# Second layer of a four-layer kernel: probability transposes one projection later, a round's maxima in one run

## The reference

```python
q = hidden_state @ Wq + bq
k = encoder_hidden_state @ Wk + bk
v = encoder_hidden_state @ Wv + bv
...
scores = jnp.einsum('bkgld,bksd->bkgls', q, k) * scale
scores = scores + encoder_attention_mask[:, :, None, :, :]
attn = jax.nn.softmax(scores, axis=-1)
out = jnp.einsum('bkgls,bksd->bkgld', attn, v)
out = out.transpose(0, 3, 1, 2, 4).reshape(b, l, H)
out = out @ Wo + bo
x = out + hidden_state
mu = jnp.mean(x, axis=-1, keepdims=True)
var = jnp.var(x, axis=-1, keepdims=True)
return (x - mu) * jax.lax.rsqrt(var + EPS) * gamma + beta
```

## Time and profile before

| | us |
|---|---|
| median of 3 runs (2545.39 to 2549.48) | 2548.41 |
| the profiled execution | 2544.39 |
| its span, first to last instruction | 2542.4 |
| PE busy, share of the span | 2443.8 (96%) |
| POOL busy | 1125.3 (44%) |
| DVE busy | 1239.3 (49%) |
| ACT busy | 1088.3 (43%) |
| layer 1, from S1 of the first pass to S1 of the last | 331.28 |

### The profile page before, as it was taken

How to read it: one execution, slowest core, us unless ns; L and a number is a source line. 1 busy time by engine, 2 the same in 40 slices (tenths; PEclk the granted TensorE clock), 3 DMA queues, 4 the chain that set the end, 5 groups by cost and what they waited for, 6 DMA issues and landing times.

```text
span 2542.4 us, 48703 instructions
## 1 busy us (share of the span) xinstructions
PE 2443.8 (96%) x18464; PEld 2046.0 (80%) x18464; DVE 1239.3 (49%) x3296; ACT 1088.3 (43%) x3712; POOL 1125.3 (44%) x1972
## 2 busy tenths in 40 slices
PE   7999999999999999998888999999999999999999
PEld 6888887888888878886777788888888888788887
DVE  5565656323224667666666332233555555432332
ACT  5555554111114877877767111112555555211111
POOL 3444435600053787778877630033345433740000
PEclk9999999999999999998999999999999999999999
DMA  4121212311033223323443320122122111330100
GB/s 158 65 67 60 93 42 84 96 50 50 8 104 126 99 82 126 111 82 124 156 155 121 116 91 7 44 92 71 35 71 72 51 51 51 104 100 1 50 34 17
DMA packets 106774, 198.07 MB, mean 78 GB/s; under 512 B 8304, under 2 KB 35632, under 8 KB 103600
## 3 DMA queue, kind: packets, MB, share of 16 engines
q1 hardware_dynamic: 106544, 194.97, 22.8%
HBM read 136.22 MB, written 58.72 MB: 77 GB/s over the span
## 4 chain that ended last, share of the span: by engine, by line
PE 76%; ACT 11%; DVE 6%; POOL 4%; DMA 2%; issue 1%; SPq 0%; DVEq 0%; POOLq 0%
PE banks L327 68%; ACT plain_high L743 5%; PE banks L468 5%; PE banks L498 3%; ACT plain_low L743 2%; POOL plain_high L1372 2%; ACT plain_work L808 1%; DVE stats L1152 1%; DVE neg_max L1026 1%; PE banks L522 1%; ACT plain_work L727 1%; DMA plain_work<-mlp_w 1%; POOL plain_low L1372 0%; POOL rounded_high L318 0%; DMA plain_high<-attention_w 0%
## 5 line engine op out<-in xcount | busy, mean ns | idle before, releaser
L327 PE MATMUL banks<-rounded_work,rounded_low 128*128 128x512 f32 (+1 forms) x2688 | 531.9, 354 | 10.4 <-DVE rounded_low L1184 8.8
L327 PEld LDWEIGHTS banks<-rounded_work,rounded_low 128*128 128x128 f32 x2688 | 444.1, 198 | 74.8 <-issue 13.8
L836 ACT ACTIVATE plain_work<-banks,columns 128x512 f32<-128x512 f32 x192 | 132.4, 690 | 862.8 <-PE banks L327 856.5
L327 PE MATMUL banks<-rounded_work,rounded_high 128*128 128x512 f32 (+1 forms) x2400 | 479.4, 353 | 1.4 <-DMA rounded_work<-ctx_split 1.1
L327 PEld LDWEIGHTS banks<-rounded_work,rounded_high 128*128 128x128 f32 x2400 | 393.7, 189 | 66.1 <-issue 4.9
L1341 DVE CAST rounded_work<-plain_work 128x512 fp32r<-128x512 f32 x192 | 104.5, 544 | 683.9 <-ACT plain_work L836 669.4
L1372 POOL TENSOR_SCALAR plain_high<-plain_high,inv_sum 128x128 f32<-128x128 f32 (+1 forms) x768 | 297.9, 413 | 303.8 <-DVE inv_sum L1044 303.4
L327 PE MATMUL banks<-rounded_low,rounded_work 128*128 128x512 f32 x1728 | 416.1, 392 | 0.0
L327 PE MATMUL banks<-rounded_high,rounded_work 128*128 128x512 f32 (+1 forms) x1728 | 391.5, 378 | 1.7 <-DVE rounded_work L1343 1.7
L327 PEld LDWEIGHTS banks<-rounded_low,rounded_work 128*128 128x128 f32 x1728 | 321.5, 188 | 70.5 <-issue 4.4
L327 PEld LDWEIGHTS banks<-rounded_high,rounded_work 128*128 128x128 f32 x1728 | 308.9, 188 | 64.5 <-issue 5.0
(11 more groups left out here) (106 smaller groups left out, 3120.2 us busy)
## 6 DMA issues: line engine op xcount, KB each, us to landing
plain_work<-x SPq DMA_DIRECT2D x96, 256.0 KB, 3.0
plain_work<-mlp_w SPq DMA_DIRECT2D x96, 256.0 KB, 2.7
rounded_work<-ctx_split SPq DMA_DIRECT2D x16, 1024.0 KB, 5.7
u<-plain_work SPq DMA_DIRECT2D x48, 256.0 KB, 2.1
plain_work<-u SPq DMA_DIRECT2D x12, 1024.0 KB, 7.0
x<-plain_work SPq DMA_DIRECT2D x48, 256.0 KB, 2.2
plain_work<-attention_w SPq DMA_DIRECT2D x44, 256.0 KB, 2.7
ctx_split<-rounded_work SPq DMA_DIRECT2D x8, 1024.0 KB, 5.6
```

What stands on the lines that cost most here:

```text
L327: mm = pe.matmul(dst, lhs(i), rhs(j), start=first and n == 0, stop=last and n == 2, skip_group_check=True)
L836: act.activation(gelu[:, j % 2, :], bank(key), ACT.Gelu_apprx_tanh, bias=col(m.y, 28 + j)).then_inc(evac_of(key), 1)
```

## The change

It rewrites the order within a pass of layer 1 on PE, ACT, DVE and SP; no instruction is added or removed, apart from where waits stand.

On PE each T stands one projection further behind the scores: between the scores that precede it and T there is now an output projection or a projection to layer 2's values, and behind T, before its A, stand the keys or queries. The wait for the next pair's rows moves from the keys to the queries, which read them. On DVE the four maxima of a round run together, the copies of the older round's banks 1 and 3 come behind the inversion of the first two sums, and the inversion of the last two comes last. On ACT the copies of banks 0 and 2 move behind the exponentials of r = 1 and r = 2. The evacuation of X, keys and queries moves with PE's order. On SP the next context is loaded at the end of a pass, behind VG, instead of at the start of the next behind VC1.

```diff
+        def pe_rows(pe, y, p):
+            for i in range(2):
+                wait_evac(pe, ("X", y.n, p, i))
...
             for p in range(PAIRS):
                 more = p + 1 < PAIRS
                 pe_scores(pe, y, p, 1)
+                if p:
+                    pe_out(pe, y, 2 * p - 1)
                 pe_turn_probs(pe, y, p, 0)
                 pe_turn_x(pe, *((y, p + 1) if more else (L[2], 0)))
-                if p:
-                    pe_out(pe, y, 2 * p - 1)
+                if more:
+                    pe_keys(pe, y, p + 1, 0)
                 pe_attend(pe, y, p, 0)
                 if more:
-                    pe_keys(pe, y, p + 1, 0)
                     pe_keys(pe, L[2], p + 1, 0)
                 pe_scores(pe, y, p, 2)
+                if more:
+                    pe_values(pe, L[2], p + 1, 0)
                 pe_turn_probs(pe, y, p, 1)
                 pe_queries(pe, *((y, p + 1) if more else (L[2], 0)), 0)
-                if more:
-                    pe_keys(pe, L[2], p + 1, 1)
                 pe_attend(pe, y, p, 1)
                 pe_scores(pe, y, p, 3)
+                if more:
+                    pe_values(pe, L[2], p + 1, 1)
                 pe_turn_probs(pe, y, p, 2)
                 if more:
-                    pe_values(pe, y, p + 1, 0)
-                    pe_values(pe, L[2], p + 1, 0)
+                    pe_keys(pe, L[2], p + 1, 1)
...
                 pe_attend(pe, y, p, 2)
                 if more:
-                    pe_scores(pe, y, p + 1, 0)
-                else:
-                    pe_scores(pe, L[2], 0, 0)
+                    pe_values(pe, y, p + 1, 0)
+                pe_scores(pe, *((y, p + 1) if more else (L[2], 0)), 0)
+                pe_out(pe, y, 2 * p)
                 pe_turn_probs(pe, y, p, 3)
...
+        def act_late_round(act, y, p, k, turned, beside, of):
+
+            act_exp(act, y, p, k, 0)
+            beside()
+            act_exp(act, y, p, k, 1)
+            act_probs(act, of, *turned, 0)
+            act_exp(act, y, p, k, 2)
+            act_probs(act, of, *turned, 2)
+            act_exp(act, y, p, k, 3)
...
+        def dve_late_round(dve, y, p, k, turned, beside, behind, of):
+            for r in range(4):
+                dve_max(dve, y, p, k, r)
+            beside()
+            dve_invert(dve, y, p, k, (0,))
+            dve_probs(dve, of, *turned, 1)
+            dve_probs(dve, of, *turned, 3)
+            behind()
+            dve_invert(dve, y, p, k, (1,))
...
+                dve_late_round(dve, y, p, 1, (p, 0), odd_out, odd_moments, y)
+                for i in range(2):
+                    dve_x(dve, *((y, p + 1) if more else (L[2], 0)), i)
...
+                dve_late_round(dve, y, p, 3, (p, 2), second_values, nothing, y)
...
                 if more:
-                    sp_keys_ahead(sp, p + 1)
+                    sp_ahead(sp, p + 1)
+                if far:
+                    wait_filled(sp, ("V", 1, p + 1, 0))
+                    sp_c(sp, y, p + 2)
```

More of the change, by code:

```diff
@@ L350, in pe_inputs @@
                 pe.wait_ge(c_loaded, 16 * (c_index(y, p) + 1))
-                wait_evac(pe, ("X", y.n, p, 0))
-                wait_evac(pe, ("X", y.n, p, 1))
+                if y.kind == LATENT:
+                    pe_rows(pe, y, p)
+        def pe_rows(pe, y, p):
+            for i in range(2):
+                wait_evac(pe, ("X", y.n, p, i))
         def pe_turn_x(pe, y, p):
@@ L391, in pe_queries @@
                 pe_inputs(pe, y, p)
+            if y.kind == GQA and i == 0:
+                pe_rows(pe, y, p)
             x_t = XT_C if y.kind == CROSS else XC[:, :, :, 2 * P:4 * P]
@@ L1034, in dve_probs, with dve_invert @@
             dve_copy(dve, ("T", y.round(p, k), r), prob_t(y)[:, r, :])
-        def dve_invert(dve, y, p, k):
+        def dve_invert(dve, y, p, k, halves=(0, 1)):
             R, u = y.round(p, k), y.use(p, k)
-            for half in range(2):
+            for half in halves:
                 for r in (2 * half, 2 * half + 1):
@@ L1167, in dve_out, with dve_added @@
             dve.tensor_tensor(hidden[:, b % 2, :], bank(key), hidden[:, b % 2, :], ALU.add).then_inc(evac_of(key), 1)
-            wait_evac(dve, key)
+        def dve_added(dve, y, b):
+            wait_evac(dve, ("out", y.n, b))
             dve_moments(dve, y, b)
+        def dve_out(dve, y, b):
+            dve_add(dve, y, b)
+            dve_added(dve, y, b)
         def dve_again(dve, y, b):
@@ L1254, in dve_gqa, with odd_out, odd_moments, again @@
             dve.wait_ge(m_stored, 64 * GROUPS)
+            dve_values(dve, L[2], 0, 1)
             for p in range(PAIRS):
                 more = p + 1 < PAIRS
-                def inputs():
-                    for i in range(2):
-                        dve_x(dve, *((y, p + 1) if more else (L[2], 0)), i)
-                def next_inputs():
-                    if not more:
-                        for i in range(2):
-                            dve_x(dve, L[2], 1, i)
-                dve_values(dve, L[2], p, 1)
-                dve_round(dve, y, p, 1, (p, 0), inputs)
-                if p:
-                    dve_again(dve, y, 2 * p - 2)
-                    dve_out(dve, y, 2 * p - 1)
+                def odd_out():
+                    if p:
+                        dve_add(dve, y, 2 * p - 1)
+                def odd_moments():
+                    if p:
+                        dve_again(dve, y, 2 * p - 2)
+                        dve_added(dve, y, 2 * p - 1)
+                def again():
+                    if p:
+                        dve_again(dve, y, 2 * p - 1)
+                def second_values():
+                    if more:
+                        dve_values(dve, L[2], p + 1, 1)
+                dve_late_round(dve, y, p, 1, (p, 0), odd_out, odd_moments, y)
+                for i in range(2):
+                    dve_x(dve, *((y, p + 1) if more else (L[2], 0)), i)
+                if more:
+                    dve_keys(dve, y, p + 1, 0)
                 dve_heads(dve, y, p, 0)
                 if more:
-                    dve_keys(dve, y, p + 1, 0)
                     dve_keys(dve, L[2], p + 1, 0)
-                dve_round(dve, y, p, 2, (p, 1), nothing)
-                if p:
-                    dve_again(dve, y, 2 * p - 1)
+                dve_late_round(dve, y, p, 2, (p, 1), nothing, again, y)
                 dve_queries(dve, *((y, p + 1) if more else (L[2], 0)), 0)
+                dve_heads(dve, y, p, 1)
+                dve_late_round(dve, y, p, 3, (p, 2), second_values, nothing, y)
                 if more:
                     dve_keys(dve, L[2], p + 1, 1)
-                dve_heads(dve, y, p, 1)
-                dve_round(dve, y, p, 3, (p, 2), nothing)
-                if not more:
+                else:
                     dve_mask(dve, L[2], 0)
@@ L1287, in dve_gqa @@
                 dve_heads(dve, y, p, 2)
-                dve_round(dve, *((y, p + 1) if more else (L[2], 0)), 0, (p, 3), nothing, y)
-                next_inputs()
-                dve_out(dve, y, 2 * p)
+                dve_late_round(dve, *((y, p + 1) if more else (L[2], 0)), 0, (p, 3), lambda: dve_add(dve, y, 2 * p),
+                               lambda: dve_added(dve, y, 2 * p), y)
                 if more:
                     dve_queries(dve, y, p + 1, 1)
+                else:
+                    for i in range(2):
+                        dve_x(dve, L[2], 1, i)
                 dve_heads(dve, y, p, 3)
@@ L1675, in sp_gqa @@
             sp_ahead(sp, 0)
+            wait_filled(sp, ("V", 2, 0, 1))
+            sp_c(sp, y, 1)
             for p in range(PAIRS):
@@ L1686, in sp_gqa @@
                 if not more:
-                    wait_filled(sp, ("V", 2, p, 1))
+                    wait_filled(sp, ("Q", 1, p, 1))
                     sp_cross_keys(sp, 0)
```

54 lines of the change are left out of this document (23 added, 31 removed).

## The result

The changed kernel takes 2553.24 us (2549.87 to 2555.11) against 2546.27 (2541.89 to 2549.48) of the kernel before, timed with it: a ratio of 1.0030, 95% interval 1.0021 to 1.0039, some 7 us slower. The forecast was +3.6, the range held the time, and of the three chances the one that came true is "slower by over 0.2%", to which I had given 0.33.

The account below looks back on a forecast made before the run. PE was taken as the bound, with gaps from waits for POOL, DVE and ACT. Six passes +0.9, first pass +2.7 and last pass 0 gave +3.6 us: 2548.0, or 2552.0 on the runs' scale (+0.14%), range 2541 to 2560.

Parts of the forecast that it names:

- The links: Prices of steps between engines in a pass, each from one row, such as 0.72 us from ACT's copy to PE's matmul.
- the ledger: One full pass timed from S0 along PE, ACT and DVE: waits sum to 3.6 us, the pass to 47.65.
- A full pass: Layer 1's six full passes: waits exchanged for waits, 47.65 against 47.53 us, +0.1 each, +0.9 in six.
- The sum of 44.1: PE's work without waits in a full pass, 44.1 us, leaving at most 3.4 to gain from 47.53.
- half the bank waits vanish: Full passes: DVE or ACT catch up sooner than the priced steps say; 10.8 us off, 2541; chance 0.14.
- ACT, which copies T late, takes its place: Full passes: the softmax chain is hidden and ACT's late copies hold PE instead; +0.1 us a pass.
- First pass: Layer 1's first pass: X waits 3.05 us, A0 falls behind KG, the clock falls once; +2.7 us.
- The loss of clock: First pass: one fall of the granted clock behind the wait ahead of X, 1.1 to 1.9 us, taken as 1.5.
- The turn to layer 2: Last pass: Q0's lateness set against T3's lost POOL wait and earlier evacuations; 0, bounds -3.0 and +4.4 us.
- the step on SP: Context load behind VG, 18 us ahead of the next KG for a transfer of 5.7; no price.
- The rival in which it falls in every pass: Granted clock falls at KG or Q0's wait in each pass; +7 to +11 us, 2559 to 2563; chance 0.13.
- That transposes don't count as busy in the same way: Skill's rule, by which every pass would start KG at the low clock; given a small chance, since a row disagreed.

Follow-up runs that it names:

- Experiment 1: The changed kernel with ACT copying T0's bank 2 and T1's bank 0 one row of exponentials earlier; ratio 1.0016 to the kernel before.
- experiment 4: The changed kernel with the last pass in its old order on PE, ACT and DVE; ratio 1.0020 to the kernel before.
- experiment 2: The changed kernel with round 1 of the first pass in its old order, A0 ahead of KG; ratio 1.0015 to the kernel before.
- experiment 6: The changed kernel with DVE's copy of T's bank 1 again between the second and third maximum; ratio 1.0293 to the kernel before.
- experiments 1 to 4: Four variants of the changed kernel: early ACT copies 1.0016, old first-pass order 1.0015, layer 2's values loaded ahead of second keys 1.0013, old last-pass order 1.0020.
- experiment 5: The changed kernel with early ACT copies, X evacuated earlier, maxima ahead of evacuations in rounds 2 and 3, VC1 copied earlier; 2532.55 us, 0.9954 to the kernel before.

## Why the prediction came out as it did

**The links were right.** With S0 at 0, the ledger put KG at 18.15, Q0 at 30.7, T2's r = 3 at 40.3 and KC1 at 40.95; they stand at 18.07, 30.82, 40.42 and 40.99 (from S0 at 896.49). T no longer waits for POOL, and PE waits for ACT's copies in front of Q0 (1.33, forecast 1.4), KG (0.98, forecast 0.65) and for heads in front of O (0.69, forecast 0.75; the view calls it issue). Q1's wait of 0.1 and KC1's of 0.2 don't show.

**A full pass, +0.1 forecast, +0.34 measured.** The term that was mis-sized is the work between the waits, 44.59 where I had 44.1, more than the waits, which sum to 3.28, forecast 3.6. I took 2.97 for KC and Q from rows where another projection stood on one side of them; alone, between T or A and A or S, they take 3.05 to 3.07 (917.22 to 920.28), which makes 12.22 for the four instead of 11.88. The four T take 7.62 instead of 7.20, as only T0 is as short as the row that I read; X and the two O take 0.5 less. The sum of 44.1 was too low for the kernel before as well, where PE is busy for 44.78 a pass and for 44.87 in the one of the earlier trace rows: there were 2.75 us of waits to lose and not 3.4, and I set a pass that was added up against one that was measured. Six passes gave +2.06 instead of +0.9.

**The price of a wait.** The rival "half the bank waits vanish" counted each as time won, to be decided by Q0's wait being under 0.7. Experiment 1 made that wait zero and won nothing. My ledger walked along ACT and DVE and so came within 0.22 of the pass, but "ACT, which copies T late, takes its place" is not the cause: late copies are one of two paths. The Trainium skill (Perfetto Trace Analysis, Optimization Strategies) advises, when the matmul engine idles, to optimize the engines that block the critical path; the traces agree only if the whole path is meant and not the releaser that the wait names.

**First pass, +2.7 forecast, +3.3 measured.** The mechanism came as written: X waits 2.85 (forecast 3.05), KG starts with the context, 7.95 behind S1 (8.06 before), A0 behind it. KG's 2.93 instead of 1.69 is 1.24 of it, A0 to its follower 1.70, KC0 0.1, and 0.28 falls behind S2. The loss of clock was taken as 1.5 and is 1.24 + 0.69 = 1.9, 0.69 being what A0 takes longer (1.77 instead of 1.08). KC0's 0.1 is not clock: in the full passes, at 1.00, it takes as long.

**The turn to layer 2, 0 forecast, +1.6 measured.** Q0 of the last pass stands 18.90 behind S1, forecast 18.95, and as forecast most of that lateness is made good behind it: up to layer 2's Q it is +0.46, inside the bounds and by experiment 4 within what the clock does there. What failed is the step on SP: I followed the context load and forgot the loads behind the layer's end. The values of layer 2 are queued behind the second keys, which wait for X of that pair; the change evacuates that X later, the values go out at 1197.27, 0.25 ahead of Q instead of 1.91 (1191.24 of 1193.15 before), and A waits 1.07.

**The clock.** The rival in which it falls in every pass didn't come. In every full pass T0, X and KG's wait of 0.98 stood together, 3.8 us without another kind of matmul, the granted clock was 1.00 over all six, and KG takes 1.66. That transposes don't count as busy in the same way (the Trainium skill, TensorE: Matmul & The Clock Gate, Part 4) would, as the prediction read it, have made KG slow in each; the trace disagrees. The clock did fall behind waits of 2.85 (the changed kernel), of 1.83 and 1.86 (experiment 2) and, in most places, of 2.6 (experiment 6).

What stays open: why experiments 1 to 4 all come out at 1.0013 to 1.0020 where the changed kernel, timed apart from them, had 1.0030, with passes equal to 0.04 us; a step of that size between two timings can't be excluded. Also open is which of the moves of experiment 5 its gain needs.

## What to carry to other kernels

Before a wait is priced, follow the chain of work for one whole period of the loop: if the waiting engine has a small part of it, 30% here, removing its waits may only move them, as in experiment 1. Where two paths join again in each round, cut both in the same round, and look also for lateness that no wait of the bound engine shows, such as maxima that stand behind an evacuation although the scores are there (here it was only cut together with banks that came free late). And where a layer's last pass is reordered, follow the queue that loads for the next layer to its end.

## Not expected of the hardware

A projection of 24 matmuls of 256 takes 2.94 to 2.97 us to the next start with another projection on one side, 3.05 to 3.07 alone between T or A and A or S: in these rows a projection that stands alone costs 0.1 more.

The six passes repeat to 0.2 us (287.21, 287.23, 287.30, 287.40 and 287.42 in five kernels of equal passes), but a stretch in which the clock can fall does not. At the start of layer 2's MLP, the same code in all, PE waits for DVE once; in the changed kernel it is this row:

```profile
1440.80 5.35 PE L327 MATMUL banks<-rounded_high,rounded_work 128*128 128x512 f32 x12 [3.90 <-DVE rounded_work L1380]
```

And in the kernel before:

```profile
1434.69 2.98 PE L327 MATMUL banks<-rounded_high,rounded_work 128*128 128x512 f32 x12 [1.66 <-DVE rounded_work L1343]
```

The granted clock over the projection is 0.53 in the first row and 1.00 in the second. In the profiles of both kernels and of the twelve experiments the wait is 1.43 to 3.90 us. In the seven where it is at most 1.95 the projection behind takes 2.97 to 3.01; in the seven from 2.11 up it takes 4.57 to 5.35. So a wait of 2.11 instead of 1.95 comes with 1.6 more behind it, which may be part of why medians of kernels with equal passes differ by 0.1%.
